# First MLP of two transformer blocks moved into the slots of the first attention, one image behind

## What is computed

```python
# layer 0 (layer 1 the same, window 16x16, head dim 48, gelu approximate=True)
xn = layer_norm(x, norm1_w, norm1_b)
q, k, v = heads(windows(pad(xn)) @ qkv_w + qkv_b)
attn = softmax(q * scale @ k.T + rel_h + rel_w)
x = x + unwindow(attn @ v) @ proj_w + proj_b
h = gelu(layer_norm(x, norm2_w, norm2_b) @ fc1_w + fc1_b, approximate=False)
x = x + h @ fc2_w + fc2_b
```

## Time and profile before

| | us |
|---|---|
| median of 3 runs (870.06 to 875.1) | 873.86 |
| the profiled execution | 873.07 |
| its span, first to last instruction | 871.2 |
| `a0`: projection of image 0 begins / of image 7 ends | 93.35 / 355.9 |
| first matmul of `m0`'s up / of `a1`'s Q and K | 358.59 / 437.65 |
| `a1`: first scores / add of image 7 | 459.3 / 794.7 |

### The profile page before, as it was taken

One profiled execution on the slowest core, in us unless ns is written; L12 is line 12 of the kernel. 1 busy time (PEld: TensorE's weight loads), 2 busy tenths in 40 slices (PEclk: granted clock), 3 DMA queues, 4 the chain that ended last, 5 costly groups with the idle time before them and its releaser, 6 DMA issues.

```text
span 871.2 us, 18544 instructions
## 1 busy us (share of the span) xinstructions
PE 768.9 (88%) x6570; PEld 616.6 (71%) x6570; DVE 534.5 (61%) x1592; ACT 436.6 (50%) x1421; POOL 128.0 (15%) x243
## 2 busy tenths in 40 slices
PE   3679889898998977779979999999999999997998
PEld 2556657575675644678866887878787878766887
DVE  6156777757677677465425576756666666674552
ACT  2035565656556555444434555555556555554432
POOL 7200111101111010141330101010101010101111
PEclk9999999989999997799996999999999999999999
DMA  7312621010210100100040404040404040400001
GB/s 145 70 35 35 156 35 23 14 31 6 37 20 17 26 11 1 37 1 1 2 72 1 75 1 74 2 74 1 74 1 75 1 75 2 75 0 1 20 20 36
DMA packets 39147, 30.06 MB, mean 34 GB/s; under 512 B 12662, under 2 KB 37010, under 8 KB 39056
## 3 DMA queue, kind: packets, MB, share of 16 engines
q1 hardware_dynamic: 36030, 26.55, 16.2%
q0 software_dynamic: 2048, 1.89, 1.2%
q10 hardware_dynamic: 978, 0.43, 0.3%
HBM read 8.77 MB, written 1.57 MB: 12 GB/s over the span
## 4 chain that ended last, share of the span: by engine, by line
PE 71%; DVE 16%; issue 4%; ACT 3%; DMA 2%; POOL 2%; SPq 1%; ACTq 1%; DVEq 0%; POOLq 0%
PE bank L1270 10%; PE bank L526 7%; PE bank L1356 7%; PE bank L1297 5%; PE bank L1145 5%; PE bank L1277 4%; PE bank L976 4%; PE bank L952 4%; PE bank L1316 4%; PE bank L1077 3%; PE bank L1412 3%; DVE Pb L704 3%; DVE xhat L432 2%; PE bank L1003 2%; PE bank L506 2%
## 5 line engine op out<-in xcount | busy, mean ns | idle before, releaser
L693 ACT ACTIVATE Pb<-bank,nmax 128x256 f32<-128x256 f32 (+1 forms) x432 | 192.4, 453 | 90.0 <-DVE nmax L683 87.2
L683 DVE TENSOR_REDUCE nmax<-bank 128x2 f32<-128x392 f32 (+2 forms) x240 | 138.7, 579 | 45.7 <-PE bank L1270 34.0
L704 DVE TENSOR_SCALAR Pb<-Pb,rsum 128x196 f32<-128x196 f32 (+2 forms) x432 | 136.2, 353 | 8.5
L723 ACT COPY area<-bank 98x392 f32<-98x392 f32 (+1 forms) x144 | 77.5, 539 | 84.3 <-PE bank L1277 72.8
L1270 PE MATMUL bank<-QK 80*128 80x256 f32 x384 | 108.2, 407 | 10.6 <-DMA QK<-rel_dense 7.9
L1270 PEld LDWEIGHTS bank<-QK 80*128 80x128 f32 x384 | 69.2, 198 | 32.1 <-issue 16.5
L693 ACT ACTIVATION_READ_ACCUMULATOR Pb<-bank,nmax 128x1 f32 x432 | 87.4, 202 | 0.0
L976 PE MATMUL bank<-ident,Pb 128*98 128x128 f32 x384 | 63.4, 290 | 20.0 <-DVE Pb L704 19.9
L515 ACT ACTIVATE area<-bank,fc1b 128x256 f32<-128x256 f32 x96 | 45.2, 476 | 58.8 <-PE bank L506 51.3
L526 PE MATMUL bank<-fc2w,area 128*128 128x192 f32 x384 | 66.4, 332 | 0.0
L976 PEld LDWEIGHTS bank<-ident,Pb 128*98 128x98 f32 x384 | 41.2, 132 | 34.3 <-DVE Pb L704 29.1
(11 more groups left out here) (151 smaller groups left out, 1481.6 us busy)
## 6 DMA issues: line engine op xcount, KB each, us to landing
QK<-dense SPq DMA_DIRECT2D x32, 288.0 KB, 6.2
QK<-dense SPq DMA_DIRECT2D x48, 64.0 KB, 2.4
QK<-dense SPq DMA_DIRECT2D x90, 28.0 KB
QK<-rel_dense SPq DMA_DIRECT2D x32, 48.0 KB, 3.3
QK<-rel_dense POOLq DMA_DIRECT2D x32, 48.0 KB, 3.0
out<-x_all SPq DMA_DIRECT2D x8, 192.0 KB, 2.0
x_all<-in_x SPq DMA_DIRECT2D x1, 1344.0 KB, 16.6
QK<-in_c_hot SPq DMA_DIRECT2D x2, 384.0 KB, 5.1
```

What stands on the lines that cost most here:

```text
L683: nc.vector.tensor_reduce(nmax[0:sc.shape[0], u % 3, 0:sc.shape[1]], sc, AX.X, ALU.max, negate=True).then_inc(self.m_rdy, 1)
L693: nc.scalar.activation(Pb[u % 3][0:rows, t, 0:cols], sc[:, t, :], ACT.Exp, bias=nmax[0:rows, u % 3, t:t + 1], accum_out=esum[0:rows, u % 3 ...
L704: nc.vector.tensor_scalar(Pb[u % 3][0:rows, t, 0:keep], Pb[u % 3][0:rows, t, 0:keep], rsum[0:rows, u % 3, t:t + 1], None, ALU.mult).then_i ...
L723: copy(*self.pt_views(u)).then_inc(self.pt[self.pt_engine(u)], 1)
```

## The change

- `m0` becomes `Mlp0`. During `a0`'s image k (1 to 7) the slots also carry the MLP of image k-1, each step after the slot's own instructions: DVE's statistics in slot 4, its normalization in slot 7; in slot 11 PE's transposes and the scaled copies and low parts of ACT and DVE; on PE up's blocks 0 and 1 in slot 12, 2 and 3 in slot 13, 4 and 5 in slot 14 and then down; all six Gelus on ACT in slot 14; DVE's add in slot 15. POOL's 1/sigma lies within the next image's front, its sum with the bias ahead of `xbias`.
- Up uses the two banks `G_BANK`, two blocks in each, so blocks 4 and 5 wait for the Gelus of 0 and 1. Down uses `O_BANK`, so values of the third group wait for DVE's add. The hidden units have a tile of their own (`hT0`), and so has the sum (`xbias_mlp`).
- After `a0`'s last image comes the whole front of `a1`'s image 0, with nothing beside it until, behind its V, the transposes of the MLP of image 7; that MLP's up and down stand on PE behind the first three scores of `a1`, and its Gelus on ACT ahead of `a1`'s first exponential. `m0.run`, `Mlp.start` for `m0` and `Attention1.start` are not called any more.
- `a0`'s small operands move from `early` into the K half of the `QK` tiles and a spare tile, so the split weights have room of their own. The fc1 weights of layer 0 are split after image 0 of `a0` (ACT and DVE), those of second attention after images 2, 3 and 4 (ACT and POOL), DVE's tables after images 3 and 4, the fc1 weights of layer 1 after image 5 (ACT and POOL; before: at the start of `a1`).
- SP loads the first MLP's weights (12 DMAs) after `a0`'s first image, everything else (29 DMAs) after its second.

The waits that guard shared buffers are left out below where they name something long past.

```diff
+        mlp0 = chunks(fc1w[0], a["L0_conv_fc1_w"]) + norm_chunks(1, "L0_conv_norm2_w", "L0_conv_norm2_b")
+        mlp0 += [(fc2w[0][:], a["L0_conv_fc2_w"].rearrange("(m p) n -> p m n", p=P)),
+                 (fc1b[0][:], col(a["L0_conv_fc1_b"], NM, p=P)), (fc2b[0][:], bcast(a["L0_conv_fc2_b"]))]
+        chunked = chunks(wq1, a["L1_conv_wq"]) + chunks(wk1, a["L1_conv_wk"]) + chunks(wv1, a["L1_conv_wv"])
...
+        class Mlp0(Mlp):
+
+
+            attention, following = None, None
+
+            def up_bank(self, m):
+                return G_BANK[(m // 2) % 2][:, (m % 2) * T:(m % 2 + 1) * T]
+
+            def dve_xhat(self, eng, n):
+                eng.wait_ge(self.norm.rstd, n.at(1, 1))
+                if n.at(1, 0) < B - 1:
+                    eng.wait_ge(self.attention.g_rdy[1], min(n.at(5, 11), 5 * B))
+                else:
+                    eng.wait_ge(self.following.g_rdy[1], 1)
+                self.norm.write_xhat(n)
+
+            def pe_norm(self, eng, n):
+                for b in range(2):
+                    if n.at(1, 0) < B - 1:
+                        eng.wait_ge(self.attention.g_out[b], self.attention.G_OUTS[b] * min(n.at(1, 3), B))
+                    else:
+                        eng.wait_ge(self.following.g_out[b], self.following.G_OUTS[b])
...
+            def pe_up(self, eng, n, blocks):
+                for m in blocks:
+                    if m == 0:
+                        eng.wait_ge(self.xl, n.at(2, 2))
+                    if n.at(1, 0) == 0 and m % (NM // 2) == 0:
+                        eng.wait_ge(self.wlo, 1 + m // (NM // 2))
+                    if m == 4:
+                        eng.wait_ge(self.g, n.at(NM, 2))
+                    for i, (w, x) in enumerate(five(fc1s[0], slice(m * P, (m + 1) * P), xns, slice(0, T))):
+                        mm = nc.tensor.matmul(self.up_bank(m), w, x, start=(i == 0), stop=(i == 4))
+                    mm.then_inc(self.h, 1)
+
+            def act_up(self, eng, n):
+                for m in range(NM):
+                    eng.wait_ge(self.h, n.at(NM, m // 2 * 2 + 2))
+                    if m == 0 and n.counts(1, 0):
+                        eng.wait_ge(self.y, n.at(1, 0))
+                    nc.scalar.activation(hT0[:, m, :], self.up_bank(m), self.func,
+                                         bias=fc1b[0][:, m:m + 1]).then_inc(self.g, 1)
+
+            def pe_down(self, eng, n):
+                if n.at(1, 0) < B - 1:
+                    eng.wait_ge(self.attention.ao[0], n.at(9, 15))
+                    eng.wait_ge(self.attention.ao[1], n.at(3, 5))
+                else:
+                    eng.wait_ge(self.attention.done, B)
+                for t in range(NT):
+                    for m in range(NM):
+                        if t == 0:
+                            eng.wait_ge(self.g, n.at(NM, m + 1))
+                        mm = nc.tensor.matmul(O_BANK[:, t * C:(t + 1) * C], hT0[:, m, t * P:(t + 1) * P],
+                                              fc2w[0][:, m, :], start=(m == 0), stop=(m == NM - 1))
+                mm.then_inc(self.y, 1)
...
+            def pe_slot(self, eng, n, u):
+                if u == 11:
+                    self.pe_norm(eng, n)
+                elif u == 12:
+                    self.pe_up(eng, n, (0, 1))
+                elif u == 13:
+                    self.pe_up(eng, n, (2, 3))
+                elif u == 14:
+                    self.pe_up(eng, n, (4, 5))
+                    self.pe_down(eng, n)
+
+            def act_slot(self, eng, n, u):
+                if u == 11:
+                    self.act_norm(eng, n)
+                elif u == 14:
+                    self.act_up(eng, n)
+
+            def dve_slot(self, eng, n, u):
+                if u == 4:
+                    self.norm.dve_stats(eng, n)
+                elif u == 7:
+                    self.dve_xhat(eng, n)
+                elif u == 11:
+                    self.dve_norm(eng, n)
+                elif u == 15:
+                    self.dve_down(eng, n)
...
+                        if mlp and has_prev:
+                            {"pe": mlp.pe_slot, "act": mlp.act_slot, "dve": mlp.dve_slot}[which](eng, n.prev(), u)
+                    if after:
+                        after(eng, n)
...
+                    if mlp and n.at(1, 0) > 1:
+                        self.pool_front(eng, n, lambda: mlp.norm.pool_rstd(eng, n.prev().prev()))
+                    else:
+                        self.pool_front(eng, n)
...
+                    elif mlp:
+                        mlp.norm.pool_rstd(eng, n.prev())
+                    if mlp and has_prev:
+                        mlp.pool_back(eng, n.prev())
                     self.pool_xbias(eng, n)
+                    if after:
+                        after(eng, n)
                 image_loop(eng, step)
...
+                if q == 2 and n.counts(1, 0):
+                    eng.wait_ge(self.mlp.done, n.at(1, 0))
...
+        def act_weights(act, n):
+            i = n.at(1, 0)
+            if i == 0:
+                act.wait_ge(ld_mlp0, 16 * len(mlp0))
+                m0.act_weights(act)
+            elif 2 <= i <= 4:
+                act.wait_ge(ld_chunked, 16 * len(chunked))
+                whole, high, _ = attention1_weights[i - 2]
                 nc.scalar.copy(high, whole).then_inc(w1_high, 1)
-
-        def pool_weights1(pool, n):
-            if weights_at(n) is not None:
-                whole, high, low = attention1_weights[weights_at(n)]
-                pool.wait_ge(w1_high, weights_at(n) + 1)
+            elif i == 5:
+                act.wait_ge(ld_later, 16 * len(later))
+                m1.act_weights(act)
+
+        def pool_weights(pool, n):
+            i = n.at(1, 0)
+            if 2 <= i <= 4:
+                whole, high, low = attention1_weights[i - 2]
+                pool.wait_ge(w1_high, i - 1)
                 nc.gpsimd.tensor_tensor(low, whole, high.bitcast(F32), ALU.subtract).then_inc(w1_low, 1)
-
-        def dve_tables1(dve, n):
-
-            if n.pair == 0:
+            elif i == 5:
+                m1.low_weights(pool, nc.gpsimd)
+
+        def dve_weights(dve, n):
+            i = n.at(1, 0)
+            if i == 0:
+                m0.low_weights(dve, nc.vector)
+                dve.wait_ge(ld_mlp0, 16 * len(mlp0))
+                dve.wait_ge(low_rows_set, 2)
+            elif i in (3, 4):
                 dve.wait_ge(prep_dve, 4)
-                for instruction in spread(nc.vector, 2 + n.par):
+                for instruction in spread(nc.vector, i - 1):
                     instruction.then_inc(relw_done, 1)
+            elif i == 5:
+                dve.wait_ge(ld_chunked, 16 * len(chunked))
+                dve.wait_ge(ld_later, 16 * len(later))
...
+            a0.run(pe, "pe", pe_meanwhile, {2: tables}, mlp=m0)
+            FIRST = Img(0, 0)
+            a1.pe_transpose_x(pe, FIRST)
+            pe.wait_ge(w1_low, 3)
+            for g in range(NPAIR):
+                a1.pe_qk(pe, FIRST, g)
+            pe.wait_ge(relw_done, H + W)
+            a1.pe_rel(pe, FIRST)
             stage_start(pe, 1)
-            pe.wait_ge(ld_later, 16 * len(later))
-            pe.wait_ge(ld_chunked, 16 * len(chunked))
-            m0.run(pe, "pe", following=lambda e, part: a1.start(e, "pe", m0, part))
-            pe.wait_ge(relw_done, H + W)
-            pe.wait_ge(w1_low, 3)
+            pe.wait_ge(prep_pool, 3)
+            for t in range(NT):
+                a1.pe_v(pe, FIRST, t)
+            m0.pe_norm(pe, LAST)
             pe.wait_ge(ld_rows1, 16 * len(rows1))
-
-            def v_space(pe):
-                stage_start(pe, 2)
-                pe.wait_ge(prep_pool, 3)
-            a1.run(pe, "pe", started=True, before_v=v_space, following=lambda e, part: m1.start(e, "pe", a1, part))
+            for u in range(3):
+                a1.pe_scores(pe, FIRST, u)
+            m0.pe_up(pe, LAST, range(NM))
+            m0.pe_down(pe, LAST)
+            a1.run(pe, "pe", started=True, following=lambda e, part: m1.start(e, "pe", a1, part))
...
+            a0.run(act, "act", between={2: loaded, 7: scatter_first}, mlp=m0, after=act_weights)
+            FIRST = Img(0, 0)
+            a1.act_xn(act, FIRST)
+            for g in range(NPAIR):
+                a1.act_q(act, FIRST, g)
+            a1.act_rel(act, FIRST)
+            for t in range(NT):
+                a1.act_v(act, FIRST, t)
+            m0.act_norm(act, LAST)
+            m0.act_up(act, LAST)
+            a1.run(act, "act", started=True, following=lambda e, part: m1.start(e, "act", a1, part))
...
+            a0.run(dve, "dve", dve_meanwhile, {0: constant_keys, 2: tables, 6: zeros_there}, mlp=m0, after=dve_weights)
+            FIRST = Img(0, 0)
+            a1.dve_stats(dve, FIRST)
+            a1.dve_xhat(dve, FIRST)
+            a1.dve_xn(dve, FIRST)
+            m0.norm.dve_stats(dve, LAST)
+            for g in range(3):
+                a1.dve_k(dve, FIRST, g)
```

(9 more changed lines are left out.)

188 lines of the change are left out of this document (95 added, 93 removed).

## The result

The changed kernel takes 876.9 us (median of 20 runs, 872.9 to 882.3), the kernel before 872.0 beside it (20 runs, 868.8 to 881.2): ratio of the means **1.0052, 95% interval 1.0028 to 1.0075**. It is slower by 0.5%, +4.5 us in the mean; forecast were +6.2. The profiled execution took 880.07 us, its span 878.2, so it lies in the upper part of the runs; PE is busy 88% of it, as before, and ACT 51%, with 18 table loads instead of 4.

The account below looks back on a forecast made before the run. PE was taken as nearly the bound in a0, 4.15 us an image open. Stage removed -81.7; added +61.5, +3.5, +7, +7.6, +2.0, +0.3, +7.0; clock -1: +6.2, so 880.0 us, range 864 to 892.

Parts of the forecast that it names:

- last image: a0's image 7, with the previous image's MLP but no next front: +3.5 us, from 1 to 9.
- An image, 10.25: Each of a0's images 1 to 6 grows by 10.25 us, 8.1 of it PE's MLP work; 61.5 for six.
- The waits of slots 4 and 14: PE waits for DVE's statistics, +0.9 us, and for load and Gelus before up's block 4, +1.6, per image.
- the waits of 0.18 and 0.77: PE's existing waits in a0, filled while DVE and ACT catch up during the MLP: -0.95 us an image.
- The small ones of slots 7, 11 and 15: PE waits from DVE's normalizations (+0.1 us), the transposes-to-up chain (+0.2) and DVE's add (+0.3), per image.
- Clock, -1: Denser PE work in a0's images may avoid the half clock of one image: 1 us less.
- Weights: Weight splits and table products moved behind a0's images: +7 us, from 3 to 12; +2.3 each after images 3 and 4.
- Head: a1's first front, uncovered: +7.6 us of idle PE from last projection to Q/K, then +2.0 for half clock.
- MLP of image 7: Up and down on PE between a1's first scores and first transposes: +7.0 us, from 4 to 10.
- Drain: Rival: each of 7 Gelu waits in slot 14 costs 1.38 us more for ACT's table switch: 889.7 us, chance 0.05.
- The MLP fills PE's gaps: Rival: Gelus ready in time and statistics in DVE's waits, 7.75 us an image: 862.5 us, chance 0.2.
- The POOL lock: Rival: in-order DVE, held by slot 11's norm and blocked by POOL behind images, sets the pace: 892 us, chance 0.17.

Follow-up runs that it names:

- e1: The changed kernel measured again without any edit, as the mark for the other runs: ratio 1.0057 to the kernel before.
- e5: Changed kernel with DVE's table products moved from behind images 3 and 4 into slot 14: 7.6 us less than the changed kernel, ratio to before 0.997.
- e10: Changed kernel with the norm of a1's first image begun in slots 14 to 17 of a0's last image: 8.5 us less, ratio to before 0.996.
- e2: Changed kernel with the first MLP's Gelu replaced by the identity, so no table loads there: 7.9 us less, ratio to before 0.9966.
- e3: Changed kernel with the MLP's statistics on DVE in slot 5 instead of slot 4: 6.4 us less, ratio to before 0.9984.
- e4: Changed kernel with slot 14's table load and six Gelus on ACT ahead of unit 16's exponentials: ratio to before 1.0058, no gain.
- The four edits: Changed kernel with statistics in slot 5, table products in slot 14, a1's first norm in slots 14 to 17, Gelus first: 847.4 us, ratio to before 0.9707.

## Why the forecast came out right

The total did, 4.5 us measured against 6.2; one part of it by two errors that cancel. Measured numbers are of the first profiled execution after, in brackets of the second one (e1).

| step | forecast | measured |
|---|---|---|
| ahead of projection 0 | +1.8 | +1.0 (+0.5) |
| six images and their weights | +61.5 + 5.2 = 66.7 | +68.3 (+68.6) |
| last image | +3.5 | +3.6 (+3.2) |
| the rest: stage away, head, MLP of image 7, clock | -65.8 | -65.9 (-69.3) |

- **An image, 10.25.** The undisturbed one is e1's image 2: no half clock and no table products, 46.48 us, so **+9.3**. The waits of slots 4 and 14 were right (+0.90, and 1.54 for 1.6), and the waits of 0.18 and 0.77 were filled as forecast. The small ones of slots 7, 11 and 15 (0.1, 0.2, 0.3) don't appear: slots 11 to 13 ran without any wait over 0.3. All waits from 0.3 up make 5.40 instead of 3.68, +1.7, so 7.6 is left for PE's work, where I had 8.1. Where the 0.5 went (overlap in the records, or small gaps that it filled) isn't shown.
- **Clock, -1.** This is the step of the sum that failed, in its sign: it stands in the last row of the table, but the time it speaks of is that of the images. Six images at 46.48 make 278.9; they took 292.8 in e1. Of the 13.9 more, 4.4 are the table products' waits; nearly all of the other 9.5 goes with the 27 us at half clock in these images (0.35 us for each). In the kernel before, the same remainder is 224.2 - 6 x 37.14 = 1.3. So half clock cost 8 us more, where I had expected denser work to avoid some, and it made up for the 5.5 us by which six images were too dear. That the total came out is luck to this extent.
- **Weights.** 2.3 for image 3 were 49.02 - 46.48 = 2.5, in an image at full clock. Here the mechanism was named too, POOL's low part blocking DVE's products, and e5 bears it out. The 0.3 for ACT's and POOL's parts alone don't appear: e1's image 2 has those of the first weights in it (POOL's low part at 186.80), and every wait in it is that of the other images. Image 0: 1.0 instead of 1.8.
- **Head.** 7.6 was 7.1, and e10 gives it back. The half clock around it was 17 us long in one execution and 7 in the other (424 to 441, 430 to 437), which is most of the difference between -65.9 and -69.3. Of Q and K 4.6 and 3.0 us ran in it, where I had 4; that it would reach the projection ahead (4.18 us instead of 2.19 in the first execution) I had not seen.
- **MLP of image 7.** a1's transposes lie 15.9 - 7.0 = 8.9 us further behind the scores, 7.0 were forecast, inside its bounds.
- **Drain.** No such time stands in the rows, 0.01 us from load to Gelu; the forecast without it was right, and e2 measures it: 7.9 us (9.7) for loads and all. The Trainium skill (ScalarE: Activation LUTs, What ACT_TABLE_LOAD costs) has the 1283 ns of the load, which the trace shows; its drain is not there.
- **The rivals.** "The MLP fills PE's gaps" decides at a wait under 0.3 in slot 14: it was 1.54. Yet e3 and e4 show how near that was: one slot for the statistics, and one order of two steps on ACT for half of the Gelu wait (0.71 stays). The POOL lock bound where it was put, and nowhere else; PE had no wait over 1 us between slots 11 and 13.

So the gain of the vanished stage (17 us without PE work) and of the filled gaps was spent on four waits and on clock: 7 x 1.54, 7 x 0.9, 2 x 2.2 and 7.1 us, 28.6 in all. The four edits take away 23.6 of them (the Gelu wait only by 0.83) without touching what is computed, and reach 847.4 us, 30.5 less; the rest goes with the 27 us less at half clock in the images.

## What to carry to other kernels

When work of one stage is laid into the slots of another, its own length on the bounding engine is easy to size and rarely the surprise; look at each in-order neighbour for what its new step stands ahead of, and put it where that engine idles in the trace (DVE had 4.7 to 7.7 us in slot 14, and the table products and the next norm stood elsewhere). Moving it was worth the whole wait here, and such waits added up. Judge a gain under 1% with the granted clock beside it, at best over many runs, and see where the half clock lies, as its mean alone doesn't say what it costs: a correct removal of 5.8 us of waits showed as nothing alone and as 12 us or more in company.
